# Ball block: the bias of the first feed-forward product is added by ScalarE instead of VectorE

## The reference, cut to what matters

```python
def plin(x, w, b):
    return expmap0(logmap0(x) @ w + b)
...
        xn = layer_norm(logmap0(x))
        xm = expmap0(xn * (1 + sc_mlp) + sh_mlp)
        ff = plin(plin(xm, w_f1, b_f1), w_f2, b_f2)
        ff_t = g_mlp * logmap0(ff)
        return mobius_add(residual, expmap0(ff_t))
```

## Time and profile before

| what | value |
|---|---|
| median of 3 runs | 3349.69 us |
| profiled execution: own time | 3347.58 us |
| its span | 3345.8 us |
| PE busy | 3143.7 us (94%) |
| DVE busy | 2103.9 us (63%) |
| ACT busy | 1706.6 us (51%) |
| POOL busy | 561.0 us (17%) |

### The profile page before, as it was taken

One profiled execution on the slowest core, in us unless ns is written; L12 is line 12 of the kernel. 1 busy time (PEld: TensorE's weight loads), 2 busy tenths in 40 slices (PEclk: granted clock), 3 DMA queues, 4 the chain that ended last, 5 costly groups with the idle time before them and its releaser, 6 DMA issues. The chain is left out here.

```text
span 3345.8 us, 53623 instructions
## 1 busy us (share of the span) xinstructions
PE 3143.7 (94%) x18984; PEld 1776.7 (53%) x18984; DVE 2103.9 (63%) x6476; ACT 1706.6 (51%) x3219; POOL 561.0 (17%) x696
## 2 busy tenths in 40 slices
PE   7999999999997688988999768999999999999998
PEld 3455555555554333443444545666666666666665
DVE  3233343343346567788876757777777777777783
ACT  2243443433433366655656335666666666666662
POOL 0000000000002334444432221111111111111110
PEclk8999999999998799999999889999999999999999
DMA  5110101101100200000001020000000000001000
GB/s 192 58 54 28 60 34 53 67 32 42 61 10 14 87 8 9 7 16 14 14 10 41 25 113 17 20 23 23 23 23 23 23 23 29 29 30 31 23 27 27
DMA packets 77619, 120.75 MB, mean 36 GB/s; under 512 B 10067, under 2 KB 65944, under 8 KB 72232
## 3 DMA queue, kind: packets, MB, share of 16 engines
q1 hardware_dynamic: 77352, 117.31, 10.3%
HBM read 96.27 MB, written 16.83 MB: 34 GB/s over the span
## 5 line engine op out<-in xcount | busy, mean ns | idle before, releaser
L651 PE MATMUL ps<-shared 128*128 128x512 f32 x768 | 375.7, 613 | 8.9 <-DMA sb<-in_sb 7.4
L2674 PE MATMUL ps<-shared 128*128 128x512 f32 x768 | 375.2, 612 | 0.0
L1260 ACT ACTIVATE shared<-ps 128x2048 f32<-128x2048 f32 x128 | 240.4, 1878 | 246.9 <-PE ps L1779 246.3
L667 PE MATMUL ps<-shared 128*128 128x512 f32 x768 | 361.9, 593 | 0.0
L2257 POOL TENSOR_TENSOR shared<-shared 128x16 f32<-128x16 f32 x64 | 186.5, 2915 | 1004.6 <-DVE shared L2460 1004.6
L1195 POOL TENSOR_TENSOR b_routs<-b_rins,b_expo 128x4 f32<-128x4 f32 x88 | 90.4, 1027 | 1375.9 <-DVE b_rins L1414 1375.9
L2714 PE MATMUL ps<-w_xnT,w_w 128*128 128x512 f32 (+1 forms) x704 | 317.3, 593 | 2.6 <-DVE w_xnT L2523 1.4
L2286 ACT ACTIVATE w_pr<-w_sm,w_nmx,shared 128x256 f32<-128x256 f32 (+1 forms) x512 | 287.1, 568 | 1.1 <-DVE w_nmx L2441 0.3
L667 PEld LDWEIGHTS ps<-shared 128*128 128x128 f32 x768 | 145.9, 191 | 185.2 <-issue 180.9
L2714 PEld LDWEIGHTS ps<-w_xnT,w_w 128*128 128x128 f32 (+1 forms) x704 | 132.2, 188 | 151.6 <-issue 146.4
L651 PEld LDWEIGHTS ps<-shared 128*128 128x128 f32 x768 | 138.3, 192 | 137.7 <-issue 120.5
(11 more groups left out here) (308 smaller groups left out, 6060.7 us busy)
## 6 DMA issues: line engine op xcount, KB each, us to landing
shared<-in_ew SPq DMA_DIRECT2D x32, 1024.0 KB, 6.7
shared<-xs SPq DMA_DIRECT2D x16, 512.0 KB, 3.9
shared<-xs SPq DMA_DIRECT2D x64, 128.0 KB, 4.2
shared<-in_xT SPq DMA_DIRECT2D x14, 512.0 KB, 5.0
shared<-x SPq DMA_DIRECT2D x9, 512.0 KB, 4.4
xres<-in_x SPq DMA_DIRECT2D x32, 128.0 KB, 2.2
x<-x1t SPq DMA_DIRECT2D x32, 128.0 KB, 1.7
b_mod<-ada SPq DMA_DIRECT2D x16, 256.0 KB, 3.1
```

Of the source, the lines that this page charges most:

```text
L651: ins = te.matmul(ps[:, G % 2], w1[:, k, j % M1 * P:(j % M1 + 1) * P], xT[:, b % 2, k], start=(k == 0), stop=(k == KD - 1))
L667: ins = te.matmul(ps[:, 2 + c], w2[:, j % M1, c * P:(c + 1) * P], hid[:, G % 4], start=(j == 0), stop=(j == J - 1))
L1260: a.activation(pr[:, G % 2], ps[:, SC:SC + 4], ACT.Exp, scale=DH ** -0.5).then_inc(p_ok, 1)
L2674: ins = te.matmul(to, hT[:, i % 2, k, t * P:(t + 1) * P], wqkv[:, i // B, k, s * 512:(s + 1) * 512], start=(k == 0), stop=(k == KD - 1))
```

## The change

The bias is added by ScalarE: an activation with the function Identity and the bias as an operand of one number for each partition, in place of VectorE's tensor_scalar. It stands at the very end of ScalarE's step, behind the tangents (`hyperbolic`) and logarithms (`logarithm`) of that step; the waits and the semaphore that it raises are the same as VectorE's were.

```diff
@@ scalar_steps
+        def hidden(b, m):
+            if b == 0 and m == 0:
+                act.wait_ge(ld_f, 4 * 16)
+            filled(act, f"f{m}", b)
+            if b:
+                filled(act, "y3", b - 1)
+            a.activation(fT[:, m], bank(f"f{m}", b), ACT.Identity, bias=bf1[:, m:m + 1]).then_inc(done(f"f{m}", b), 1)
...
             if at(G, 53) is not None:
                 hyperbolic(at(G, 53), th2_ask, th2_ok)
+            if among(G, F1):
+                for m in among(G, F1)[1]:
+                    hidden(among(G, F1)[0], m)
@@ vector_steps
-        def hidden(b, m):
-            if b == 0 and m == 0:
-                dve.wait_ge(ld_f, 4 * 16)
-            filled(dve, f"f{m}", b)
-            if b:
-                filled(dve, "y3", b - 1)
-            v.tensor_scalar(fT[:, m], bank(f"f{m}", b), bf1[:, m:m + 1], None, ALU.add).then_inc(done(f"f{m}", b), 1)
...
-            if among(G, F1):
-                for m in among(G, F1)[1]:
-                    hidden(among(G, F1)[0], m)
             if rows_due(G):
```

## The result

| kernel | median | runs | ratio to before, 95% interval |
|---|---|---|---|
| before | 3349.93 us | 4 runs, 3345.21 to 3350.57 | |
| after | 3315.78 us | 4 runs, 3312.43 to 3318.84 | 0.9902 [0.989, 0.9915] |

The change makes the kernel about 1% faster, 34 us by the medians. The prediction was 3314.0.

A forecast was written before the change was run, and what follows sets the result against it. TensorE, busy 499.2 of 545 us, was taken to set the pace, waiting mostly on VectorE's queue. Waits of 29.3 us plus 4.2 in the tail gave 33.5 off 3347.6, so 3314 us; range 3298 to 3336.

The forecast's parts named there:

- the clock: Granted clock 0.97 over the attention stretch, 16 us missed; a gain of 0 in the sum, up to 8 in the range.
- TensorE's waits in the stretch: 1300 to 1845 us, attention beside feed-forward: 29.3 us of TensorE's waits won, range ends 16.2 and 40.7.
- The direct waits: TensorE's waits at the sum with the bias itself, 1300 to 1845 us: all 16.2 us go.
- The attention's result: TensorE's waits for the attention's transposed result, 12.5 us in the stretch: 7.1 us won.
- VectorE's lead of 5.1 against 4.4 us: At the attention's result in one entry: VectorE gains 5.1 us, TensorE would come 4.4 us earlier, so it suffices.
- The keys: TensorE's waits for VectorE's copy of the keys, 4.9 us in the stretch: 4 won, part of one long wait may stay.
- the second product's row: TensorE's waits for this row from VectorE, 7.1 us in the stretch: about half go, new ones come, so 2 won.
- Rival A: Only the direct waits go, as other work keeps VectorE late: 18 us won with half the tail, 3329 us; chance 0.21.
- The costs on ScalarE: 0.687 us per addition, at most 1.38 a pair, fitting ScalarE's idle 2.30 to 3.00 us before the Exps at steps 37, 39, 41.
- rival C: Slower: sums push the Exp, 24 pairs cost 33 us while 16.2 are won, +17, 3365 us; chance 0.05.
- VectorE's 7.9 us per entry: Per entry VectorE gains 5.6 us of additions and 2.3 of standing for the first product, against TensorE's 8.87 of waits.
- The tail: 1845 to 1984 us, feed-forward of the last two entries: 4.2 us from three pairs of entry 6, bounds 0 and 10.

The follow-up runs named there:

- middle pairs: Half of the change: f2 to f5 (steps 39 and 41) added by ScalarE, f0, f1, f6, f7 by VectorE as before; 3335.35 us, 0.9966 of before.
- stand-in kernels: Changed kernel plus an unused same-shape sum on VectorE at each addition's old place: 3342.41 us; with VectorE also waiting for the product there: 3356.73 us.
- the two halves: Only half of each entry's pairs moved to ScalarE, against before: second and third pair 3335.35 us; first and last pair 3327.33 us.
- keys' copy alone: Kernel before, addition left on VectorE, but its copy of the keys made by ScalarE; 3340.97 us, 0.9981 of before.
- slower stand-in: Changed kernel plus an unused sum on VectorE at each addition's old place, with VectorE waiting for the product first; 3356.73 us, 1.0034 of before.
- the first one: Changed kernel plus an unused sum on VectorE at each addition's old place, without a wait for the product; 3342.41 us, 0.9989 of before.
- the last kernel: Changed kernel with ScalarE's sum at the front of its step in the last two entries, and the keys' copy on ScalarE; 3303.63 us, 0.9874 of before.
- a second relief of 12 us on VectorE: Changed kernel with the copy of the keys moved to ScalarE as well; 3312.96 us, 0.99 of before.

## Why the prediction was right, and where it was not

*The sum.* Predicted -33.5 us against the profiled execution, measured -28.7 there and 34 by the medians. The total is right, but the waits of the stretch were put 10.3 us too high and the clock, at nothing, 11.1 us too low, so the agreement of the total is in good part luck.

*TensorE's waits in the stretch.* Predicted 29.3 us, measured 19.0 less idle time. The mechanism held: VectorE's queue got shorter and the waits that end in it shrank. The direct waits (16.2) went as said. The attention's result gave back 11.1 (12.5 to 1.4) where 7.1 were taken: VectorE's lead of 5.1 against 4.4 us held at nearly every such place. The keys, taken as a gain of 4, lost 3.4 (4.9 to 8.3), and the second product's row, taken as a gain of 2, lost 2.2 (7.1 to 9.3). The step that failed is "Keys: 4.9, less one long wait that may stay in part, 4", and with it that for the row. TensorE, no longer held at the sum, comes to these jobs earlier, and VectorE has its chain of narrow work in front of them. The Exp's wait rose from 4.3 to 6.0, and waits for `b_y` (1.2) are new.

*The clock.* Counted 0 in the sum, although the prediction saw the fall to 0.59 behind a wait, and up to 8 in the range. The matmuls of the stretch took 11.1 us less. This term was the mis-sized one with the most weight. In the table, busy time and clock go with the idle time: 26.8 us idle and 488.1 busy at 0.99; 40.3 and 500.7 at 0.96 with waits of up to 5.2 us; 52.3 and 500.5 at 0.95. The middle pairs, also 40.3 us idle, have 495.4 at 0.97, so idle time alone doesn't fix the clock.

*Rival A (only the direct waits, 3329)* rested on the direct waits as a gain of their own. That was the main error of thought. The stand-in kernels have no direct wait in the stretch, and a gain of 3 us or a loss of 11. These 16.2 us were one place at which a late VectorE showed; freed there alone, it shows at the next.

*The costs on ScalarE.* 0.687 us was taken, 0.686 was measured (median of 64). The Exp was hardly pushed: rival C, 3365, fails. The prediction took 2.30 us as the least cover and named step 39 as the tightest place, without TensorE being faster; after the change the Exp that had 3.00 us of idle time in front of it in the earlier trace rows has 0.22, and at two other places nothing is left, so this cover is used up.

*VectorE's 7.9 us per entry.* The term of the prediction that carried the rest. The stall of 2.3 went in full (13.9 over six entries), the work of 5.6 was 4.4 net (26.4 over six), as other instructions of VectorE took longer. That work and stall both count is borne out by the two stand-ins and the two halves.

*The tail.* Predicted 4.2 us, the marks show 1.8, and with VectorE doing these sums again no difference can be told. ScalarE's queue gives back what VectorE's gains: TensorE after, from 1850 to 1930 us:

```profile
1855.78 1.98 PE L1848 MATMUL ps<-bb_uT,bb_wf 128*128 128x512 f32 x4 [1.69 <-ACT bb_fT L1333]
1871.99 6.05 PE L1864 MATMUL ps<-bb_wf,bb_fT 128*128 128x256 f32 x16 [9.07 <-ACT bb_fT L1333]
1910.82 3.70 PE L1848 MATMUL ps<-bb_uT,bb_wf 128*128 128x512 f32 x8 [1.25 <-ACT bb_fT L1333]
1916.82 7.11 PE L1848 MATMUL ps<-bb_uT,bb_wf 128*128 128x512 f32 x12 [2.29 <-ACT bb_fT L1333]
```

The prediction saw that the moved sum isn't late at steps 37 and 39 of an entry with attention, and at step 39 of entry 7, but not behind the logarithm of entry 6, nor that the last two entries have window-layer work in ScalarE's queue.

*Open.* That the keys' copy alone brought 6 and not 11 us goes with VectorE's longer stall for GpSimd's inverse roots, as the traces show, but no run tests it. Unexplained are some 2 us in the stretch of the slower stand-in, some 5 of the first one's time, and why the last kernel gained more than its two edits alone.

## What to carry to other kernels

Before adding up the waits that a change takes away, ask whose queue they all end in: waits on one late engine are one delay seen at several places, and freeing one place without shortening the queue only moves the wait. Count the stalls of the late engine together with its work, and place a moved instruction where it doesn't put a new stall in front of something that this engine needs. When the waits on a busy TensorE shrink, expect the matmuls themselves to run faster too, and ask before taking more off whether the engine would only stand where it now works: here a second relief of 12 us on VectorE came back as a longer stall for GpSimd, and brought almost nothing.

## What the runs showed of the hardware

VectorE's addition out of PSUM never took longer than its usual time, while the stand-in, with both inputs in SBUF, at times took more than twice its usual time. The addition's 64 took 735 to 753 ns. The stand-in's line in the second of its kernels (minimum/median/maximum ns):

```profile
L1647 DVE TENSOR_TENSOR bb_junkv<-bb_wf x64: 682/692/1642, 1311.7 to 1961.5; 128x512 f32<-128x512 f32 x64
```

The pair of 2.36 us above ran while GpSimd worked on 128x512 in SBUF. The Trainium skill ("SBUF — State Buffer", section "SBUF: two separate sides") says that VectorE with two inputs in SBUF and GpSimd reading SBUF exclude each other for a whole instruction; the trace agrees: the second of GpSimd's two sums started within 0.1 us of the stand-ins and took 1797 ns, the first 1265. An instruction that stands in for another's time should therefore read from the same memories, PSUM or SBUF.

The Identity with a bias for each partition, 128x512 float32 out of PSUM, takes 686 ns on ScalarE, 1.25 us for a pair back to back, against 750 ns and 1.41 us for VectorE's addition. The Copy, without a bias operand, has 588 ns. The Trainium skill ("ScalarE: Activation LUTs", section "Rules for kernel authors") sends additions to VectorE, for its rate in bf16; for this type and shape the measurement decides against it, by time of the instruction and, what weighs more here, by whose queue is late.
